# A five-layer decoder block on one core: turns from a list rule instead of fixed lags, and a memory layer with its probabilities normalised on GpSimd and its values loaded as column tiles

## The chip, the core and the metric

The kernel runs on one core of one Trainium2 chip. The metric is the device time of one execution in microseconds. Three runs of the kernel before took 1000.18, 1001.05 and 1002.54 us; their median is 1001.05 us.

## The reference, cut to what matters

```
x = x + attention(layernorm(x))                # 16 heads of 128, over the sequence: about half of the time
x = x + linear_attention(layernorm(x), ctx)    # "lin": relu features, 16 heads of 16, 64 context tokens
x = x + ffn(layernorm(x))                      # "ffn": silu, 704 hidden, 4-bit weights
x = x + feature_attention(layernorm(x))        # "fat": 256 x 256 energy, softmax
x = x + memory_attention(layernorm(x), ctx)    # "mem": the layer that the change rewrites
x = x + ternary_ffn(layernorm(x))              # "ter": 1024 hidden, relu squared, rounded to 255 steps

# memory_attention, per batch: 256 tokens, 16 heads of 16, 64 memory tokens
attn = softmax(where(mask, q @ k.T * scale, -inf))     # [16 heads, 256, 64]
out  = sigmoid(x @ wg.T) * ((attn @ v) @ wo.T)
# quantized relu2, per token: h = relu(h)**2; hmax = max(h, eps); h = round(h / hmax * 255) / 255 * hmax
```

x is 8 batches of 256 tokens of 256 features in float32.

## The kernel before, in words

The program has two parts with a barrier between them. `attention_part` does the first layer for all batches and prepares weights; it ends at about 560 us of the span. The change touches only one thing in it (two small memsets on GpSimd). `streams_part` does the other five layers. From its start on, batches don't need each other.

`streams_part` treats four batches at a time, as four streams. Each stream has buffers of its own (`xn_stream`, `xt_stream`, `big_stream`, `mid_stream` and others) and two of the eight PSUM banks, PA and PB. A loop (`Fori`) of two rounds does batches 0 to 3 and then 4 to 7. A round begins on DVE with the stage `copy` (L1392), which copies the batch from X into `x_stream`.

The order of the work is a list of stages written out by hand, one list for all layers. A stage is a small step of one batch, on one or more engines. `in_turns` goes through time slots, and in each slot the four streams come in turn, stream s being `LAGS[s]` = 0, 3, 6 or 9 slots behind stream 0. Each engine issues its own instructions in this order and waits on semaphores in it, so an instruction that waits holds up all that stands behind it on its engine. Since a round ends with the last stage of stream 3, no engine starts a stage of batches 4 to 7 before its last stage of batches 0 to 3.

The steps that the change and the prediction speak of, each per batch and, in mem and ter, per tile t of 128 tokens (two tiles for a batch, one after the other):

- norm of every layer: statistics on DVE (L1353, L1359, L1368), a power of -1/2 on GpSimd (L1222), the normalised x on DVE (L1373), four transposes on PE (L1554).
- `mem s`: two mask matmuls over 128 rows (L1670), then four score matmuls over 64 rows each (L1675); pairs of these use the upper and the lower half of the rows and write different banks.
- `mem max`, `sub` (DVE, L1479 and L1482), `exp` (ScalarE, L1304), `pt` (eight transposes on PE, L1683), `pte` (ScalarE, L1308).
- `mem o`: eight matmuls (L1689), with a 128x128 block of the probabilities as weights and 34 columns of v1 (two heads of 16, each with a column of ones for the row sum) moving.
- `mem rd`, `on` (DVE, L1486 and L1490): one over the row sum, and the product with it; then, once per batch, `mem ot` (four transposes on PE, L1554), `ote` (ScalarE, L1312) and `out` (four matmuls on PE, L1546).
- `ter h` (PE, L1704), `max` (DVE, L1498), `m0`, `m1`, `c0`, `c` (five small operations on DVE, L1502 to L1515), relu and square (ScalarE, L1317 and L1322), `r` and `n` (DVE, L1519 and L1522: round, and back to a float16 number), `nt` (PE, L1711), `nte` (ScalarE, L1326), `out` (PE, L1717), `add` (DVE, L1526).
- the output of a batch is a DMA from `x_stream` on the queue of SP (L1207).

A float32 matmul shows as two records in the trace, and so do its weight loads; the counts of L1675, L1689 and L1546 are twice the number of matmuls in the code.

## Time and profile before

| | |
|---|---|
| the profiled execution, its own time | 998.32 us |
| its span, first to last instruction | 996.5 us |
| mean granted clock of TensorE | 0.967 of 2.4 GHz |
| attention part, 0 to 560 us | not changed but for the memsets |
| streams part, 560 to 996.5 us | two rounds: the first ends at about 780 us |
| PE, DVE, ScalarE, GpSimd busy over the span | 912.4, 714.6, 506.8, 338.1 us |

The windows view cuts the streams part into stretches and gives the busy time of each engine in each. The two rounds run the same work, and their stretches can be laid side by side: 572 to 671 and 792 to 889 hold lin, ffn, fat and the start of mem, 671 to 728 and 889 to 946 the rest of mem, 728 to 780 and 946 to 996.5 the ternary layer.

### The profile page before, as it was taken

Reading aid. Unit: us, or ns where it says so; the run is one execution under the profiler, and the core shown is the slowest. Engines: PE = TensorE matmul, PEld = TensorE weight load, DVE = VectorE, ACT = ScalarE, POOL = GpSimd, SP = SyncE. Lnnn points to the kernel's source line nnn. Section 1 sums busy time; section 2 is a strip of 40 time slices with the busy share of each in tenths; the row PEclk is TensorE's granted clock in tenths of the full one; section 3 lists DMA queues with packets and bytes.
Section 4 is the critical chain, followed back from the end, with each engine's and each line's share of the span. In section 5 each row is a group of like instructions: output and inputs, shape, how many; then the busy total and the mean of one; then the engine's idle time right before and its main releaser. Section 6 shows DMA issues by size and latency. Waiting matters only on the chain. (4 is left out here: it accounts for less than half of the span.)

```text
span 996.5 us, 18805 instructions
## 1 busy us (share of the span) xinstructions
PE 912.4 (92%) x6772; PEld 685.7 (69%) x6772; DVE 714.6 (72%) x1785; ACT 506.8 (51%) x1219; POOL 338.1 (34%) x342
## 2 busy tenths in 40 slices
PE   5788999999999999999999599999877699999966
PEld 3556677777777777777777488787754488787843
DVE  6738778788887889878764447775588438775586
ACT  1445586666665666655664233533437224444455
POOL 3105455554554555554464302510010303410000
PEclk9799999999999999999999799999999699999998
DMA  8023131111001111001000000000000000000001
GB/s 270 22 61 79 21 93 33 33 32 32 8 24 32 32 32 32 8 24 32 11 1 1 1 1 2 1 1 1 1 1 22 23 1 1 1 1 1 1 1 43
DMA packets 34438, 25.27 MB, mean 25 GB/s; under 512 B 9332, under 2 KB 31436, under 8 KB 34380
## 3 DMA queue, kind: packets, MB, share of 16 engines
q1 hardware_dynamic: 34092, 24.23, 9.1%
q8 instruction: 36, 0.59, 0.2%
q10 hardware_dynamic: 288, 0.26, 0.1%
q14 instruction: 22, 0.18, 0.1%
HBM read 22.32 MB, written 2.17 MB: 25 GB/s over the span
## 5 line engine op out<-in xcount | busy, mean ns | idle before, releaser
L73 PE MATMUL banks<-value_out_hi,xn_t_hi 128*128 128x256 f16 x512 | 140.3, 274 | 2.3 <-DVE X L837 2.3
L572 ACT ACTIVATE exp_scores<-banks,exp_bias,unscale 128x256 f32<-128x256 f32 x256 | 141.0, 560 | 2.1
L468 POOL CAST exp_hi<-exp_scores 128x1024 f16<-128x1024 f32 x64 | 67.0, 1046 | 216.8 <-ACT exp_scores L572 216.8
L75 PE MATMUL banks<-value_out_hi,xn_t_lo 128*128 128x256 f16 x512 | 140.3, 274 | 0.0
L74 PE MATMUL banks<-value_out_lo,xn_t_hi 128*128 128x256 f16 x512 | 140.3, 274 | 0.0
L470 POOL TENSOR_TENSOR exp_lo<-exp_scores,exp_hi 128x1024 f16<-128x1024 f32 x64 | 138.3, 2160 | 5.1
L1222 POOL TENSOR_TENSOR rstd_stream<-rstd_stream,neg_half 128x2 f32<-128x2 f32 x40 | 29.5, 738 | 314.6 <-DVE rstd_stream L1368 279.2
L1009 PE MATMUL banks<-qk 128*128 128x256 f32 x512 | 121.4, 380 | 6.1 <-ACT exp_scores L572 6.0
L1009 PEld LDWEIGHTS banks<-qk 128*128 128x128 f32 x512 | 96.8, 190 | 26.7 <-issue 7.9
L837 DVE SCALAR_TENSOR_TENSOR X<-banks,colsum,X 128x256 f32<-128x256 f32 x256 | 106.2, 478 | 11.0 <-DVE colsum L828 9.6
L554 ACT ACTIVATE qk<-banks 128x512 f32<-128x512 f32 x128 | 75.8, 598 | 60.8 <-PE banks L75 60.7
L816 DVE TENSOR_REDUCE neg_rowmax<-banks 128x4 f32<-128x1024 f32 x64 | 78.2, 1222 | 29.9 <-PE banks L1009 29.9
L73 PE MATMUL banks<-xn_t_hi,head_weights_hi 128*128 128x512 f16 x256 | 96.9, 378 | 0.6 <-issue 0.6
L75 PE MATMUL banks<-xn_t_hi,head_weights_lo 128*128 128x512 f16 x256 | 97.0, 379 | 0.0
L74 PE MATMUL banks<-xn_t_lo,head_weights_hi 128*128 128x512 f16 x256 | 96.9, 379 | 0.0
L568 ACT ACTIVATE exp_bias<-neg_rowmax,unscale 128x4 f32<-128x4 f32 x64 | 18.8, 293 | 100.9 <-DVE neg_rowmax L816 100.9
L74 PEld LDWEIGHTS banks<-value_out_lo,xn_t_hi 128*128 128x128 f16 x512 | 50.3, 98 | 12.0
L73 PEld LDWEIGHTS banks<-value_out_hi,xn_t_hi 128*128 128x128 f16 x512 | 50.3, 98 | 11.2 <-DVE X L837 4.5
L75 PEld LDWEIGHTS banks<-value_out_hi,xn_t_lo 128*128 128x128 f16 x512 | 50.4, 98 | 6.0
L572 ACT ACTIVATION_READ_ACCUMULATOR exp_scores<-banks,exp_bias,unscale 128x1 f32 x256 | 50.8, 198 | 0.0
L1554 PE MATMUL banks<-ident,xn_stream 128*128 128x128 f32 x224 | 36.3, 287 | 14.3 <-DVE xn_stream L1373 14.3
L420 POOL TENSOR_TENSOR head_weights_lo<-head_weights,head_weights_hi 128x512 f16<-128x512 f32 x32 | 38.9, 1216 | 29.5 <-ACT head_weights_hi L486 29.4
(222 smaller groups left out, 1971.6 us busy)
## 6 DMA issues: line engine op xcount, KB each, us to landing
head_weights<-in_wqkv_d SPq DMA_DIRECT2D x32, 128.0 KB, 3.6
weight_absmax_rows<-across_partitions SPq DMA_DIRECT2D x15, 256.0 KB, 4.0
X<-in_x_d SPq DMA_DIRECT2D x4, 512.0 KB, 6.8
head_weights<-in_wqkvt_d SPq DMA_DIRECT2D x16, 128.0 KB, 3.4
head_weights<-in_w_o_d SPq DMA_DIRECT2D x16, 128.0 KB, 3.4
out<-x_stream SPq DMA_DIRECT2D x8, 256.0 KB, 2.1
features_then_ternary<-in_c_fc_d SPq DMA_DIRECT2D x1, 1024.0 KB, 5.6
features_then_ternary<-in_c_proj_d SPq DMA_DIRECT2D x1, 1024.0 KB, 7.3
```

What stands on the lines that cost most here:

```text
L73: nc.tensor.matmul(out, lhs[0], rhs[0], start=first, stop=False)
L74: nc.tensor.matmul(out, lhs[0], rhs[1], start=False, stop=False)
L75: return nc.tensor.matmul(out, lhs[1], rhs[0], start=False, stop=last)
L420: nc.gpsimd.tensor_tensor(wlo[:, u, 2 * a:2 * a + 2], wst[:, u, 2 * a:2 * a + 2], whi[:, u, 2 * a:2 * a + 2], ALU.subtract).then_inc(wlo_r ...
L468: nc.gpsimd.tensor_copy(probh[:, s1_.par], prob[:, s1_.par]).then_inc(exph_ready, 1)
L470: nc.gpsimd.tensor_tensor(probl[:, s1_.par], prob[:, s1_.par], probh[:, s1_.par], ALU.subtract).then_inc(expl_ready, 1)
L554: nc.scalar.activation(qk[:, st.par, s, :], qk_ps[s], ACT.Copy).then_inc(qk_ready, 1)
L572: last = nc.scalar.activation(prob[:, s1_.par, t, :], sc_ps[t // ST][:, t % ST, :], ACT.Exp, bias=nbias[:, t:t + 1], scale=unscale[:, s1_. ...
L816: nc.vector.tensor_reduce(nmax[:, :], sc_both, AX.X, ALU.max, negate=True).then_inc(nmax_ready, 1)
L837: last = nc.vector.scalar_tensor_tensor(out=g.X[:, TP * s2.p + t, :], in0=xm_ps[t // ST][:, t % ST, :], scalar=csum[:, t:t + 1], in1=g.X[: ...
L1009: last = nc.tensor.matmul(sc_ps[b][:, t, :], qk[:, s1_.par, 0, q], qk[:, s1_.par, 1, kk], start=True, stop=True)
L1554: last = nc.tensor.transpose(tiles(bank[s])[:, k, t * P:(t + 1) * P], xn[s][:, t, k * P:(k + 1) * P], g.ident[:, :])
```

## The change

Nine things are done; the first three are about order, the others about work.

1. The loop of two rounds is written out: all eight batches stand in one sequence, on all engines. Batches b and b + 4 share a set of buffers and two PSUM banks.
2. The order is no longer slots with lags but comes from `turns_by_engine`. It takes the list `work` (each step with its engine, a length written into it, and what it needs), and places the steps one by one: always the one that can start earliest by these lengths; of those that can start at the same time, the one with the longest chain still ahead of it, plus `LEAD` = 5.0 us for each stream place ahead, and with batches 0 to 3 ahead of 4 to 7. On each engine, batch b keeps behind batch b - 1 step by step, and batch b + 4 starts when the last step of batch b is done.
3. Steps that had been joined into one slot are placed one by one (in ffn above all).
4. Batches are worked on in place in X: the stage `copy` is gone.
5. mem: the probabilities are summed on DVE (`sum`, new), and multiplied by one over the sum on GpSimd (`pn`, new), before they are transposed. The column of ones in v1 and its memsets are gone.
6. mem: `o` has v1 as weights, 128x32 for two heads, and the probabilities move, 128 columns; the eight matmuls write four groups of 32 partitions of PA. So their result comes out transposed: `mem on` on DVE and `mem ot` on PE are gone. ScalarE moves it out, once per tile instead of once per batch.
7. mem: each mask matmul takes 64 rows instead of 128, one half of the rows for each bank.
8. ter: `m1`, `r` and one of the small operations' places are gone; the scale goes into the square on ScalarE, and `n` rounds and comes back in one operation with two additions.
9. SP, like the rest, waits on constants; the output DMA goes from X.

```diff
-LAGS = (0, 3, 6, 9)
+ENGINES = ("PE", "DVE", "ACT", "POOL")
+HOP, LEAD = 0.15, 5.0
...
-        for a in range(2):
-            if a:
-                pool.wait_ge(v1_ones, 1)
-            nc.gpsimd.memset(g.v1[a * M:(a + 1) * M, :, :, a, XD:XD + 1], 1.0).then_inc(v1_ones, 1)
-        pool.wait_ge(v1_ones, 2)
 
         for p in range(1, NP):
...
-    xs = sb("x_stream", [P, ST, D])
+    xs = [g.X[:, ST * b:ST * (b + 1), :] for b in R]
...
-    NORM = ["stats", "aggr", "eps", "xn", "turn", "xt", "lo"]
-    named = lambda layer, parts: [" ".join(f"{layer}_{k}" for k in p.split()) for p in parts]
...
+
+
+    NORM = ["stats", "aggr", "eps", "xn", "lo"]
+    def norm_work(layer, after, more):
+
+        return [f"{layer}_stats DVE .75 {after}", f"{layer}_aggr DVE .25", f"{layer}_eps DVE .11", f"{layer}_pow POOL .79",
+                f"{layer}_xn DVE .78", f"{layer}_turn PE .47"] + [f"{layer}_{w}" for w in more]
...
+    work += norm_work("mem", "fat_add", ["xt ACT .85"])
+    work += ["mem_q PE 1.74", "mem_kbd DVE .68 fat_add", "mem_g PE 1.74 mem_xt", "mem_qt ACT .6 mem_q", "mem_ge ACT .6 mem_g"]
     for t in range(ST):
-        stages += named(f"mem{t}", MEM_SLOTS)
-    stages += ["mem_ot", "mem_ote", "mem_out", "mem_go", "mem_add"]
-    stages += norm_stages("ter")
+        work += [f"mem{t}_{w}" for w in ("s PE 1.33" + (" mem_qt mem_kbd mem_ge" if t == 0 else ""),
+                                         "max DVE 1.17", "sub DVE 1.15", "exp ACT 1.05", "sum DVE 1.17", "rd DVE .2",
+                                         "pn POOL 2.2", "pt PE .92", "pte ACT 1.02", "o PE .75", "ote ACT .36")]
+    work += ["mem_out PE 1.74", "mem_go DVE .63", "mem_add DVE .63"]
+    work += norm_work("ter", "mem_add", ["xt ACT .6", "lo DVE .68"])
-        stages += named(f"ter{t}", TER_SLOTS)
-    stages += ["store"]
-
-    def in_turns(stage):
-
-        for slot in range(len(stages) + LAGS[-1]):
-            for s in R:
-                if 0 <= slot - LAGS[s] < len(stages):
-                    for name in stages[slot - LAGS[s]].split():
-                        layer, _, part = name.partition("_")
-                        stage(s, name, layer, part)
-
-    def numbers(eng, it):
-
-        return [eng.snap(it * STREAMS + (s + 1)) for s in R]
-
-    def tile_numbers(eng, it):
-
-        return [eng.snap(it * FFT + (m + 1)) for m in range(FFT)]
-
+        work += [f"ter{t}_{w}" for w in ("h PE 1.72" + (" ter0_nte ter0_add" if t else ""), "max DVE 1.17", "m0 DVE .2",
+                                         f"relu ACT 1.1 ter{t}_max", f"c0 DVE .3 ter{t}_m0", "c1 DVE .16",
+                                         f"sq ACT 1.05 ter{t}_relu ter{t}_c1", "n DVE .63", "nt PE .55", "nte ACT 1.01",
+                                         "out PE .87", "add DVE .42")]
+    turns = turns_by_engine(work)
+
+    def in_turns(eng, stage):
+
+        for b, name in turns[eng]:
+            layer, _, part = name.partition("_")
+            stage(b, name, layer, part)
...
+            elif part == "pn":
+                t = tile_of(layer)
+                pool.wait_ge(mem_rden[t], n[s])
+                nc.gpsimd.tensor_tensor(by_head(s), by_head(s), den[s][:, t, :].unsqueeze(2).broadcast_to([P, XH, M]),
+                                        ALU.mult).then_inc(mem_pn[t], 1)
...
+            elif layer in ("mem0", "mem1") and part == "ote":
+
+                t = tile_of(layer)
+                act.wait_ge(mem_o_full[t], n[s])
+                nc.scalar.activation(ot[s][:, :, t * P:(t + 1) * P], PA[s][:, 0:KT * P].rearrange("p (k n) -> p k n", k=KT),
+                                     ACT.Copy, scale=g.anykey[:, s:s + 1]).then_inc(mem_o[t], 1)
...
-                                                   op0=ALU.mult, op1=ALU.mult).then_inc(mem_o[t], 1)
...
-                elif part == "r":
-                    dve.wait_ge(ter_step[s], it * (5 * ST) + (5 * t + 5))
-                    dve.wait_ge(ter_sq[t], n[s])
-                    nc.vector.tensor_scalar(hid[s], hid[s], small[s][:, 8:9], ROUND, ALU.mult, ALU.add).then_inc(ter_r[t], 1)
-                elif part == "n":
-                    dve.wait_ge(ter_r[t], n[s])
-                    nc.vector.tensor_scalar(num[s], hid[s], -ROUND, None, ALU.add).then_inc(ter_n[t], 1)
...
+            elif part == "sum":
+                dve.wait_ge(mem_exp[t], n[s])
+                nc.vector.tensor_reduce(den[s][:, t, :], by_head(s), AX.X, ALU.add).then_inc(mem_sum[t], 1)
+            elif part == "rd":
+                dve.wait_ge(mem_sum[t], n[s])
+                nc.vector.reciprocal(den[s][:, t, :], den[s][:, t, :]).then_inc(mem_rden[t], 1)
...
+            elif part == "m0":
+                dve.wait_ge(ter_max[t], n[s])
+                nc.vector.tensor_scalar(small[s][:, 5:6], small[s][:, 4:5], g.tscale[:, 0:1], float(np.sqrt(1e-5)),
+                                        ALU.mult, ALU.max).then_inc(ter_step[s], 1)
+            elif part == "c0":
+                dve.wait_ge(ter_step[s], s // STREAMS * 3 * ST + 3 * t + 1)
+                nc.vector.reciprocal(small[s][:, 6:7], small[s][:, 5:6]).then_inc(ter_step[s], 1)
+                nc.vector.tensor_scalar(small[s][:, 9 + t:10 + t], small[s][:, 5:6], small[s][:, 5:6],
+                                        g.tscale255[:, 0:1], ALU.mult, ALU.mult).then_inc(ter_step[s], 1)
+            elif part == "c1":
+                dve.wait_ge(ter_step[s], s // STREAMS * 3 * ST + 3 * t + 2)
+                nc.vector.tensor_scalar(small[s][:, 7:8], small[s][:, 6:7], float(np.sqrt(255.0)), None,
+                                        ALU.mult).then_inc(ter_scale[t], 1)
+            elif part == "n":
+                dve.wait_ge(ter_sq[t], n[s])
+                nc.vector.tensor_scalar(num[s], hid[s], ROUND, -ROUND, ALU.add, ALU.add).then_inc(ter_n[t], 1)
...
+                for bank, rows in zip((PA[s], PB[s]), row_tiles):
+                    nc.tensor.matmul(bank.rearrange("p (h m) -> p h m", m=M), g.ones[rows, :],
+                                     g.maskb[rows, s:s + 1, :].broadcast_to([P // 2, HK, M]),
...
+            elif part == "o":
+                pe.wait_ge(mem_pt[t], n[s])
+                for j in range(XH // 2):
+                    rows = slice(j % 4 * 2 * XD, (j % 4 + 1) * 2 * XD)
+                    last = nc.tensor.matmul(PA[s][rows, j // 4 * P:(j // 4 + 1) * P],
+                                            g.v1[:, s, j].rearrange("p a e -> p (a e)"), pt[s][:, j * P:(j + 1) * P],
+                                            start=True, stop=True)
...
+def turns_by_engine(work):
+
+
+
+
+
+    names, engine, length, after = [], [], [], []
+    made = {}
+    for i, line in enumerate(work):
+        name, eng, took, *before = line.split()
+        names.append(name)
+        engine.append(eng)
+        length.append(float(took))
+        after.append([j for d in before or names[-2:-1] for j in made[d]])
+        made.setdefault(name, []).append(i)
+    users = [[j for j in range(len(work)) if i in after[j]] for i in range(len(work))]
+    rest = [0.0] * len(work)
+    for i in reversed(range(len(work))):
+        rest[i] = length[i] + HOP + max([rest[j] for j in users[i]], default=0.0)
+    own = {e: [i for i in range(len(work)) if engine[i] == e] for e in ENGINES}
+    urgency = lambda b, i: rest[i] + (max(rest) if b < STREAMS else 0.0) + LEAD * (STREAMS - b % STREAMS)
+    free = {e: 0.0 for e in ENGINES}
+    nth = {(b, e): 0 for b in range(B) for e in ENGINES}
+    done = {}
+    turns = {e: [] for e in ENGINES}
+    for _ in range(B * len(work)):
+        best = None
+        for b in range(B):
+            for e in ENGINES:
+                if nth[b, e] == len(own[e]):
+                    continue
+                i = own[e][nth[b, e]]
+                needs = [(b, j) for j in after[i]]
+                if b >= STREAMS:
+                    needs.append((b - STREAMS, len(work) - 1))
+                if b and nth[b - 1, e] <= nth[b, e] or any(x not in done for x in needs):
+                    continue
+                start = max([free[e]] + [done[x] for x in needs])
+                if best is None or (start, -urgency(b, i)) < best[0]:
+                    best = (start, -urgency(b, i)), b, e, i
+        (start, _), b, e, i = best
+        free[e] = start + length[i]
+        done[b, i] = free[e] + HOP
+        nth[b, e] += 1
+        turns[e].append((b, names[i]))
+    return turns
 
...
     g.kv0 = sb("kv0", [P, B, XH // 2, 34])
     g.k1t = sb("k1_t", [P, KT, B * M])
-    g.v1 = sb("v1", [P, B, XH // 2, 2, XD + 1])
+    g.v1 = sb("v1", [P, B, XH // 2, 2, XD])
```

## Rows read from the trace of the kernel before

**Rows 1.** The page, part 1: busy us and share of the span of each engine.
```profile
PE 912.4 (92%) x6772; PEld 685.7 (69%) x6772; DVE 714.6 (72%) x1785; ACT 506.8 (51%) x1219; POOL 338.1 (34%) x342
```

**Rows 2.** Windows of the streams part: busy us and count by engine, PE clock.
```profile
728.00:780.00 52.00, 34.73 (x223) 20.38 (x221) 38.20 (x102) 27.22 (x29) 2.46 (x3) 0.90 0.07 22
...
792.00:889.00 97.00, 95.70 (x685) 79.94 (x684) 66.61 (x194) 40.04 (x101) 25.62 (x37) 0.98 0.00 1
889.00:946.00 57.00, 53.81 (x373) 44.02 (x372) 32.92 (x61) 23.18 (x30) 2.06 (x3) 1.00 0.00 1
946.00:996.50 50.50, 33.67 (x216) 19.80 (x214) 37.38 (x96) 26.94 (x28) 1.95 (x3) 0.88 0.06 22
```

**Rows 3.** Timeline from one round of the loop to the next.
```profile
766.05 11.62 SPq L1207 DMA_DIRECT2D out<-x_stream  x4
...
776.64 0.48 DVE L1526 SCALAR_TENSOR_TENSOR x_stream<-banks,small_stream,x_stream 128x256 f32<-128x256 f32 x1 [3.04 <-PE banks L1717]
779.98 0.43 DVE L1392 COPY x_stream<-X 128x512 f32 x1 [2.85 <-issue]
...
783.40 1.11 PE L1554 MATMUL banks<-ident,xn_stream 128*128 128x128 f32 x4 [6.86 <-DVE xn_stream L1373]
...
785.20 3.78 PE L1539 MATMUL banks<-xt_stream,wq 128*128 128x256 f32 x8 [0.69 <-ACT xt_stream L1249]
```

**Rows 4.** Windows over the same place.
```profile
764.00:772.00 8.00, 4.62 (x39) 2.65 (x37) 6.51 (x20) 6.16 (x6) 0.00 (x0) 1.00 0.19 65
772.00:788.00 16.00, 7.34 (x35) 5.19 (x36) 7.33 (x24) 1.62 (x2) 4.08 (x4) 0.54 0.11 36
788.00:792.00 4.00, 3.93 (x19) 2.78 (x18) 2.10 (x8) 2.03 (x4) 2.16 (x3) 0.71 0.00 0
```

**Rows 5.** Timeline of a score stage, and of a turn before an output product.
```profile
671.13 0.59 PE L1670 MATMUL banks<-mask_bias,ones 128*128 x2
...
671.65 0.73 PEld L1675 LDWEIGHTS banks<-big_stream,qt_stream 64*128 64x128 f32 x8 [0.42 <-issue]
671.65 1.13 PE L1675 MATMUL banks<-big_stream,qt_stream 64*128 64x256 f32 x8
672.72 0.94 PEld L1539 LDWEIGHTS banks<-xt_stream,wq 128*128 128x128 f32 x5 [0.33 <-issue]
...
727.02 0.64 PE L1554 MATMUL banks<-ident,xn_stream 128*128 128x128 f32 x4
...
727.49 1.68 PE L1546 MATMUL banks<-wo,ot_stream 128*128 128x256 f32 x7
```

**Rows 6.** Three pieces of the chain that ended last: start, us, what.
```profile
671.72 1.06 PE banks L1675 x8
...
674.71 1.74 PE banks L1546 x8
...
683.95 1.71 PE banks L1689 x16
```

**Rows 7.** Groups of the streams part by line, and L470 from the page.
```profile
L1222 POOL TENSOR_TENSOR rstd_stream<-rstd_stream,neg_half 128x2 f32<-128x2 f32 x40 | 29.5, 738 | 314.6 <-DVE rstd_stream L1368 279.2 <-DVE rstd_stream L1365 35.4
...
L1479 DVE TENSOR_REDUCE den_stream<-banks 128x16 f32<-128x1024 f32 x16 | 19.6, 1225 | 22.2 <-PE banks L1675 22.2
...
L1519 DVE TENSOR_SCALAR big_stream<-big_stream,small_stream 128x1024 f32<-128x1024 f32 x16 | 12.0, 751 | 3.0 <-ACT big_stream L1322 2.5
...
L1233 POOL TENSOR_TENSOR x_stream<-x_stream,bo 128x512 f32<-128x512 f32 x8 | 10.8, 1350 | 9.3 <-DVE xn_stream L1373 9.3
...
L1252 ACT ACTIVATE xt_stream<-banks,normw 128x256 f32<-128x256 f32 x16 | 6.7, 472 | 0.0
...
L1490 DVE SCALAR_TENSOR_TENSOR xn_stream<-banks,any_key,den_stream 128x256 f32<-128x256 f32 x16 | 7.4, 462 | 0.0
...
L470 POOL TENSOR_TENSOR exp_lo<-exp_scores,exp_hi 128x1024 f16<-128x1024 f32 x64 | 138.3, 2160 | 5.1
```

**Rows 8.** Waits of PE in the streams part: total, times, longest.
```profile
PE banks L1554 <- DVE xn_stream L1373: 14.3, 4, 6.9
```

More of the change, by code:

```diff
@@ new lines, in streams_part @@
+    for place in range(2 * FFT + 3):
+        for back, part in enumerate(("ab PE .87", "tanh ACT .36", "u DVE .36", "h DVE .42", "hi ACT .36", "lo POOL .68")):
+            m = tile_at(place - back)
+            if m is not None:
+                name, length = part.split(" ", 1)
+                before = f"ffn_{('lo', 'ab', 'tanh', 'u', 'h', 'hi')[back]}"
+                after = f"{before}{m}" if back else "ffn_lo" if m < 2 else f"ffn_h{m - 2}"
+                work += [f"ffn_{name}{m} {length} {after}"]
@@ L1212, in _ @@
+        sp.wait_ge(stored, 16 * B)
     @block.gpsimd
     def _(pool):
[L1214 to L1236 removed]
@@ L1330, in _ @@
+        in_turns("ACT", stage)
     @block.vector
@@ L1533, in _ @@
+        in_turns("DVE", stage)
     @block.tensor
```

850 lines of the change are left out of this document (392 added, 458 removed).

## The prediction

> **What bounds the kernel now.** I read the page's busy times first. PE leads with 912.4 of 996.5 us, DVE follows with 714.6 [rows 1]. A share over the whole span says little here, since the change acts on the 436 us after 560 us alone, so I cut those into windows by layer. The reader is to see three kinds of stretch in them. In lin, ffn and fat PE is busy 95.7 of 97.0 us: PE sets the pace, DVE has a third of its time free, and no order of turns can win more than 1.3 us there. In the memory layer PE is busy 53.8 of 57.0 us and DVE 32.9: PE still sets the pace. In the ternary layer nobody is full: PE 34.7 of 52.0 and 33.7 of 50.5 us, DVE 38.2 and 37.4 [rows 2]. There each of four batches walks down a long chain, and DVE is the engine most in demand. The stretches of the other round are like these.
>
> Then I read the place between the rounds in the timeline. The first batch's output leaves at 766.05, the last add of the round is at 776.64, the copy of batch 4 begins at 779.98 (2.85 us of this wait is put down to no other engine), its first transposes at 783.40 after 6.86 us of waiting, and its query product takes 3.78 us from 785.20 [rows 3] against 1.74 us for a product of the same eight records later [rows 6]. The windows say why: the granted clock is 0.54 from 772 to 788, close to the 1.2 GHz level, and 0.71 in the 4 us after it [rows 4]. So the change of rounds costs idle time and then slow time. The waits of PE agree: 14.3 us in only 4 waits go to normalised inputs that are late, the longest 6.9 us [rows 8].
>
> **Order of turns and one sequence.** Batch 4 may start when batch 0 is done, 14 us before it does now (766.05 against 779.98), so its lin work falls into the end of the ternary layer. How much is that worth? From 764 to 792 PE is busy 4.6, 7.3 and 3.9 us at clocks of 1.00, 0.54 and 0.71 [rows 4]; at full clock that is 4.6 + 4.0 + 2.8 = 11.4 us of work in 28 us. DVE is busy 6.5 + 7.3 + 2.1 = 15.9 us there; four copies of 0.43 and about two of the removed rounding operations (0.95, below) come off, 12.3 us stay, and at 88% of DVE that is 14 us. DVE decides, and the stretch saves **14 us**. From 728 to 764 nothing overlaps yet, but six tiles drop 0.95 us of DVE each, 5.7 us; I take **4 us**. Together 18; bounds 10 (batch 0 finishes only just before batch 3, since all four go nearly in step) and 26 (DVE no limit: 28 - 11.4/0.95 = 16, and more in the ternary layer, where 17.3 of 52.0 us of PE are idle).
>
> What is queued behind what: the new order is as fixed as the old one, and on each engine an operation that is late holds up the others. I cost this at nothing in lin, ffn and fat, where PE's queue is full and hides it; with the cover gone it costs what the order places wrongly, which nothing here bounds but the 1.3 us that PE idles now on one side and the ternary layer's rate of idling (a third) on the other. The copy of the first batch was ahead of everything at 560 us: **1 us** (0.43 and a hop). The other copies were covered by PE. The two memsets of v1's ones on GpSimd lie early in the attention part with nobody waiting: 0. SP still issues eight output DMAs; only the last one counts, as now.
>
> **The memory layer on PE**, per tile, 16 tiles:
> - Values. Before: 1.71 us for eight matmuls, 0.214 us each, of which only the weight loads can be the reason, since just 34 columns move [rows 6]. After: 128 columns move; a matmul of 256 columns costs 1.74/4 = 0.43 us, so 128 cost 0.22. The trace has no column tiles, but it has row tiles: four score matmuls of 256 columns take 1.06 us where four whole ones take 1.74 [rows 6], so pairs run side by side at 2 x 0.43 + 0.20. If four column tiles do the same, eight matmuls take 2 x 0.22 + 0.3 for going in and out of the tiled form = 0.75 us, and 0.96 us are saved. If they don't, they take 8 x 0.22 + 0.3 = 2.05 and 0.34 are lost. I take the side of the row tiles, the nearest row: 16 x 0.96 = 15.4 us.
> - Turning the result: 727.49 - 727.02 = 0.47 us [rows 5], 8 times, 3.8 us.
> - Masks: two one behind the other are 671.65 - 671.13 = 0.52 us [rows 5]; side by side half, so 16 x 0.26 = 4.2 us, less the entry into the row form, which stays; 3.4 us.
> Sum 22.6 us of PE work, 11.3 us in each round's memory window.
>
> What a change of form costs stands in the same rows. The weight load of the scores waits 0.42 us, that of the next stage 0.33 us [rows 5], but the matmuls themselves start 0.52 us after the masks, where the two masks alone need 2 x 0.21, so I count 0.1 in and 0.2 out. The Trainium skill (TensorEngine Tiling (Array Packing), Key Properties) says that changing the tiling mode drains TensorE, and each value stage adds two such changes. With the whole 0.42 + 0.33 us charged, a value stage takes 0.44 + 0.75 = 1.19 us, 7 us less is saved in all, and the time would be 966 us instead of 959.
>
> **The memory layer on DVE, ScalarE, GpSimd.** DVE gains `sum`, like the maximum over 128x1024, 1.22 us, and loses the product `on`, 0.46 [rows 7]: +0.76 x 8 = 6.1 us a window, 32.9 + 6.1 = 39 us. ScalarE gains a second evacuation: one more 256-column move, at most 16 x 0.47 = 7.5 us [rows 7] even with the old one counted at nothing, on an engine half free [rows 1]. GpSimd gains `pn`, 128x1024 in float32: 2.16 us like L470 or 2 x 1.35 = 2.7 us like L1233 [rows 7]; 8 x 2.7 = 22 us in a window where it does nearly nothing. But `pn` and `sum` lie in the chain of a tile: about 1.22 + 2.7 + two hops more, about 0.96 + 0.47 less. And behind a `pn` on GpSimd's queue stand the 0.74 us powers of other batches' norms, which can be 2.7 us late. Four batches must hide a chain that is some 2.5 us longer per tile, with PE's work down to 53.8 - 11.3 = 42.5 us and DVE's at 39. PE fills 94% of this window now and 67% of the ternary one; I take 88%, nearer the first since PE is still the fullest: 42.5/0.88 = 48.3, a gain of 8.7 us, **18 us** in two rounds. Bounds 2 and 24 (42.5/0.94 = 45).
>
> **The ternary layer.** `r` (0.75 us, L1519 [rows 7]) and one small operation of about 0.2 us go from each tile's chain. In the last window DVE loses 8 x 0.95 = 7.6 us; the last batch's own chain loses 2 x 0.95 = 1.9. Between them: **5 us**, bounds 2 and 8.
>
> **Sum.** 18 + 1 + 18 + 5 = 42 us. The profiled execution took 998.32 us with a span of 996.5; 998.3 - 42 = 956.3. The median of the runs is 1001.05, 2.7 us above it, so **959 us**.
>
> **Rivals.**
> - The memory layer gives nothing, since column tiles run one by one (2.05 us a stage) or the longer chain through GpSimd starves PE. PE's work falls only by 16 x (0.21 - 0.34) + 3.8, about 2 us. 2 + 18 + 1 + 5 = 26: 975 us, 970 to 982. For it: no row shows a column tile, and DVE comes close to PE. Against: row tiles do overlap, and GpSimd idles. Chance 0.14. The drain counted in full lies between this and the forecast and is part of neither; by the rows half of it is hidden. Chance 0.08, 966 us.
> - Every place fills up: memory windows at 94% (24), the change of rounds 26, last window 8, head 1: 59 us, 942 us, 932 to 948. For it: PE's idle time now lies almost only where the four batches end or begin, and one sequence could close that. Against: a batch waits for the whole of the one whose buffers it takes. Chance 0.22.
> - No overlap between the rounds, since the order keeps the four in step and batch 0 ends late: 10 instead of 18, 967 us. Chance 0.06.
> - Slower: the clock. After 6.9 us of PE idle time the granted clock is near half, and a product takes 3.78 us instead of 1.74 [rows 3, 4]. If the lighter memory layer leaves PE gaps in which its clock falls to 1.2 GHz, the work done there takes twice as long. Each microsecond of PE work at the lower level costs one more; with 42 us gained, it decides from 42 us on, that is one of the two memory windows whole. Both whole would give 959 + 85 = 1044 us. For it: in the ternary layer, PE at 67%, the clock is 0.90 and 0.88 [rows 2]. Against: most of that fall lies at the ends of those windows, and the gaps in between are only of 1 to 3 us. Chance 0.04.
> - The forecast, 949 to 965 us around 959: chance 0.46.
>
> **How the numbers follow.** The range 940 to 980 takes in the forecast, most of both neighbours and the full drain, and leaves out some 0.16: the far side of the good rival, the end of the bad one, and the slower one. Within 0.2% (2 us) of before is no change that can be measured; faster 0.95, the same 0.01, slower 0.04.
>
> **What the profile after would show.** Value stages of 0.75 us, four matmuls side by side, and no transposes behind them; if 2 us, the tiles run one by one. `pn` at 2.2 to 2.7 us. In the memory windows PE at 85 to 90% and DVE near 80%. No idle stretch of PE above 3 us in the middle of the streams part, the clock at 1.0 there, lin work of batch 4 between ternary work of batches 1 to 3. The last window some 45 us. The prediction is wrong if the fixed order meets lengths that the chip doesn't have: then PE waits 1 us and more, often, in lin, ffn and fat too, where it has no idle time now.

## The result, and the profile after

Four runs of the changed kernel took 964.23 to 969.64 us, median 966.02; four of the kernel before on the same chip had a median of 1000.62. The ratio is 0.9656 with a 95% interval of 0.9622 to 0.969: faster by 34.6 us. The forecast was 959, with 949 to 965 for its own case and 940 to 980 for the range. It was 7 us too low, inside the range and 1 us outside its own case. The profiled execution took 967.47 us, its span is 965.7 us, 30.8 less than before.

The page's busy times answer to [rows 1]. PE's fell by 24 us, DVE's rose by 10:

```profile
span 965.7 us, 18389 instructions
PE 888.5 (92%) x6740; PEld 662.4 (69%) x6740; DVE 724.2 (75%) x1745; ACT 508.9 (53%) x1227; POOL 367.7 (38%) x356
```

To see where the time came from I cut both spans at the same events: the first score matmul of a round's memory layer, the last gated add of that layer, and the last add of the ternary layer.

| stretch | before | after | gained | forecast |
|---|---|---|---|---|
| start of the span to the first scores | 671.7 | 673.3 | -1.6 | 1 |
| memory layer, batches 0 to 3 | 65.4 | 63.7 | 1.7 | 9 |
| from there to the scores of batch 4 | 152.8 | 130.1 | 22.7 | 18 |
| memory layer, batches 4 to 7 | 63.8 | 62.1 | 1.7 | 9 |
| from there to the last ternary add | 39.5 | 33.4 | 6.1 | 5 |
| after it | 3.3 | 3.1 | 0.2 | 0 |

The windows view of the kernel after answers to [rows 2] and [rows 4]. A row gives the stretch and its length, then the busy times of PE, weight loads, DVE, ScalarE and GpSimd (with counts), the granted clock, the DMA share and GB/s; the sixth row comes from the same view with the instructions of L1565 alone and leaves the other engines out:

```profile
673.30:737.00 63.70, 53.37 (x412) 38.61 (x408) 57.34 (x97) 30.50 (x43) 19.04 (x13) 0.95 0.00 1
867.10:929.20 62.10, 51.84 (x412) 37.78 (x408) 57.17 (x96) 30.24 (x43) 19.04 (x13) 0.97 0.00 1
...
572.00:673.30 101.30, 100.74 (x688) 83.31 (x689) 64.53 (x181) 40.26 (x101) 25.50 (x37) 0.94 0.00 1
...
750.00:780.00 30.00, 27.57 (x216) 21.29 (x213) 21.30 (x66) 19.40 (x27) 6.92 (x7) 1.00 0.11 36
...
800.00:810.00 10.00, 9.69 (x50) 8.65 (x49) 4.14 (x13) 1.06 (x2) 0.70 (x1) 0.66 0.00 0
...
800.00:810.00 10.00, 5.03 (x32) 4.92 (x32) 0.66 0.00 0
```

In the memory layer the bound has changed hands. PE is at 84% and 83%, and DVE at 90% and 92%. DVE is busy 57 us between these events. Before, it was 39.6 there, and the 6.1 us that the forecast adds (to 32.9 in its shorter window) would make it 45.7. At the change of rounds the long idle time is gone: from 750 to 780 PE is busy 27.57 of 30 us at full clock.

The timeline of the kernel after shows both (start, length, engine, line and tiles; in brackets the idle time before it):

```profile
698.50 0.39 PE L1642 MATMUL banks<-mask_bias,ones 64*128 64x512 bf16 x2 [0.75 <-ACT gate_stream L1297]
698.71 1.04 PE L1647 MATMUL banks<-big_stream,qt_stream 64*128 64x256 f32 x8
...
699.68 0.64 PE L1662 MATMUL banks<-mid_stream,v 128*32 128x128 f32 x16
...
700.26 1.09 PE L1655 MATMUL banks<-ident,big_stream 128*128 128x128 f32 x8
...
709.79 1.90 POOL L1229 TENSOR_TENSOR big_stream<-big_stream,den_stream 128x1024 f32<-128x1024 f32 x1 [1.58 <-DVE den_stream L1479]
710.33 1.92 DVE L1458 SCALAR_TENSOR_TENSOR X<-gate_stream,X 128x512 f32<-128x512 f32 x1
...
728.04 1.12 PE L1534 MATMUL banks<-ident,xn_stream 128*128 128x128 f32 x4 [1.96 <-DVE xn_stream L1371]
730.57 3.59 PE L1677 MATMUL banks<-ternary,xt_stream 128*128 128x512 f16 x8 [0.41 <-DVE xt_stream L1376]
...
752.99 0.74 DVE L1351 BATCH_NORM_STATS2 stats_stream<-X 128x6 f32<-128x256 f32 x2
...
758.59 0.60 PE L1534 MATMUL banks<-ident,xn_stream 128*128 128x128 f32 x4
758.87 0.48 DVE L1506 SCALAR_TENSOR_TENSOR X<-banks,small_stream,X 128x256 f32<-128x256 f32 x1 [0.32 <-PE banks L1690]
...
760.11 1.13 PE L1519 MATMUL banks<-xt_stream,wq 128*128 128x256 f32 x4
```

A value stage (L1662) takes 0.58 us from its start to that of the next stage, where eight matmuls took 1.71 [rows 6]. Masks and scores take 1.18 us (698.50 to 699.68) against 1.59 (671.13 to 672.72 in [rows 5]). Batch 4's statistics begin at 752.99, its transposes and query product at 758.59 and 760.11, among ternary adds of the first round (L1506), the last of which begins at 776.5. Before, the copy came 3.3 us after the start of the last of them [rows 3]. And at 710.33 lies what the prediction doesn't have: a gated add on DVE takes 1.92 us, where it took 0.686 before. It ends 0.56 us after the product `pn` on GpSimd that was running when it began. This is one gated add in four; the other three of the round meet no `pn` and take 0.68.

The two lines from 728 on show a second price. A variance operation at 723.68 takes 1.27 us beside a `pn` that runs from 723.03, and the normalised x behind it is late. PE is busy only 1.19 us from 724 to 728 and 3.56 from 728 to 732. The granted clock is 0.98, then 0.50, then 0.74 until 737, and eight ternary products (L1677) take 3.59 us where the same eight at 722.20 took 1.90. Round two has the same place at 922, with 0.57 from 922 to 926.

The groups view of the streams part (total busy, mean ns of one, then the idle time before them) gives the sizes; the first two rows answer to [rows 7]:

```profile
L1229 POOL TENSOR_TENSOR big_stream<-big_stream,den_stream 128x1024 f32<-128x1024 f32 x16 | 30.4, 1907 | 48.0 <-DVE den_stream L1479 48.0
L1476 DVE TENSOR_REDUCE den_stream<-big_stream 128x16 f32<-128x1024 f32 x16 | 19.2, 1200 | 1.5 <-ACT big_stream L1301 1.5
...
L1366 DVE TENSOR_SCALAR rstd_stream<-mv_stream 128x2 f32<-128x2 f32 x32 | 11.9, 373 | 0.3
...
L1662 PE MATMUL banks<-mid_stream,v 128*32 128x128 f32 x256 | 11.2, 296 | 2.4 <-ACT mid_stream L1305 2.3
...
L1447 DVE TENSOR_TENSOR big_stream<-k_t,headmask 128x256 f32<-128x256 f32 x16 | 9.3, 620 | 0.0
L1458 DVE SCALAR_TENSOR_TENSOR X<-gate_stream,X 128x512 f32<-128x512 f32 x8 | 7.9, 991 | 0.1
```

`pn` takes 1.91 us, less than forecast. But the variance operation of 128x2 elements (L1366) has a mean of 373 ns where it had 169, the key blocks (L1447) 620 against 420, the gated add (L1458) 991 against 686: DVE instructions that the change didn't touch, all longer.

The waits of PE (total, times, longest) answer to [rows 8]:

```profile
PE banks L1534 <- DVE xn_stream L1371: 12.9, 6, 6.9
PE banks L1690 <- ACT mid_stream L1327: 8.0, 10, 1.1
PE banks L1655 <- POOL big_stream L1229: 4.1, 4, 1.2
```

The 6.9 us are now those of the start of the streams part, ending at 567.6. After it no wait of PE is longer than 1.96 us.

### The profile page after: what moved, and what is told of

It is laid out like the page before. It is cut to its first block and busy times, and to the rows that moved or that the text cites. A ratio compares the mean times of both kernels' runs of the same rounds, so it can differ in the third digit from the quotient of the medians.

```text
span 965.7 us, 18389 instructions
## 1 busy us (share of the span) xinstructions
PE 888.5 (92%) x6740; PEld 662.4 (69%) x6740; DVE 724.2 (75%) x1745; ACT 508.9 (53%) x1227; POOL 367.7 (38%) x356
## 5 line engine op out<-in xcount | busy, mean ns | idle before, releaser
L74 PEld LDWEIGHTS banks<-value_out_hi,xn_t_hi 128*128 128x128 f16 x512 | 50.3, 98 | 11.2 <-DVE X L830 4.5
L1229 POOL TENSOR_TENSOR big_stream<-big_stream,den_stream 128x1024 f32<-128x1024 f32 x16 | 30.4, 1907 | 48.0 <-DVE den_stream L1479 48.0
```

The costliest lines, as they stand in the source:

```text
L74: nc.tensor.matmul(out, lhs[0], rhs[0], start=first, stop=False)
```

## The experiments

All are edits of the changed kernel, and all ratios are to runs of the kernel before on the same chip. The median of the kernel before lay between 999.94 and 1003.25 us beside these kernels, with single runs from 994.8 to 1006.8. So differences between two kernels are given by medians, and by ratios where these say something else. A difference of a few microseconds between two kernels isn't told apart from nothing.

### Which part of the change gives how much

**The order alone.** The memory layer of before, with its own work list and lengths, in the new order; the rest as changed.

```diff
-                       "max DVE 1.17", "sub DVE 1.15", "exp ACT 1.05", "sum DVE 1.17", "rd DVE .2",
-                       "pn POOL 2.2", "pt PE .92", "pte ACT 1.02", "o PE .75", "ote ACT .36")]
-    work += ["mem_out PE 1.74", "mem_go DVE .63", "mem_add DVE .63"]
+                       "max DVE 1.17", "sub DVE 1.15", "exp ACT 1.05",
+                       "pt PE .92", "pte ACT 1.02", "o PE 1.71", "rd DVE .26", "on DVE .46")]
+    work += ["mem_ot PE .47", "mem_ote ACT .6", "mem_out PE 1.74", "mem_go DVE .63", "mem_add DVE .63"]
...
```

> The changed kernel with the memory layer of before (ones column in v1, product and turn behind the values, masks over 128 rows); order, one sequence, work in place and ternary layer as changed. Theory A (the memory layer's saving on PE is mostly lost because DVE becomes its bound, the join of the rounds gives what the prediction said): 1000.6 - 18 - 5 - 1 = 977 us, 973 to 981, so the new memory layer is worth 7 to 15 us. Theory B (the memory layer gives all of its 18 us, and the order loses elsewhere): 984 us or more. Theory C (the memory layer gives nothing): 966 to 969 us.

982.87 us (974.13 to 983.63), ratio 0.9788 [0.9726, 0.9851], between the ranges of theories A and B. In the new order the rewrite is worth 16.9 us by medians and 13 by ratios. Its window of the second memory stretch:

```profile
874.30:943.70 69.40, 66.49 (x427) 53.18 (x426) 44.82 (x94) 29.15 (x39) 3.48 (x5) 0.95 0.00 1
```

The stretch is 69.4 us long, not 63.8: the list rule brings work of the neighbouring layers into it (427 matmul records against 394 between the same events before, and 5.2 us of DVE's work), and PE is at 96%. So the table above hides the rewrite's gain: in the new order it takes this stretch from 69.4 to 62.1.

**The work alone.** The changed work in the old slots and lags, in two rounds one after the other.

```diff
-    turns = turns_by_engine(work)
+    turns = turns_by_slots(work)
+def turns_by_slots(work):
+    ...
+        slots += [f"mem{t}_{p}" for p in ("s", "max", "sub", "exp", "sum rd", "pn", "pt", "pte", "o", "ote")]
+    ...
+    lags = (0, 3, 6, 9)
+    for first in range(0, B, STREAMS):
+        for slot in range(len(slots) + lags[-1]):
+            ...
```

> The changed kernel's work, written out and in place, but its turns by the slots and lags 0, 3, 6, 9 of before, in two rounds one behind the other (sum and reciprocal, GpSimd's product and the evacuation have slots of their own). Theory A: the memory layer gives about 10, the ternary one 8 in two rounds, the copies 1, the join of the rounds nothing: 1000.6 - 19 = 982 us, 977 to 987. Theory B (the list rule hurts outside the join): 970 us or less. If the join is worth less than thought, also near 972.

987.77 us (985.02 to 988.38), ratio 0.9863 [0.9824, 0.9902], just above theory A's range: 12.2 us by the median of before beside it, 1000.01, and 13.7 by the ratio. The memory stretches are 59.9 and 58.7 us:

```profile
883.80:942.50 58.70, 47.56 (x379) 35.83 (x376) 47.20 (x77) 26.56 (x37) 18.03 (x12) 0.94 0.00 1
```

In the old slots `pn` hardly meets the operations that it holds up elsewhere: the means are 184 ns for the variance operation, 420 for the key blocks and 682 for the gated add; only the normalisation is longer, 496 against 456. DVE is at 80%, as forecast. Even so the two stretches gain only 5.5 and 5.1 us where the forecast had 8.7 each. PE is at 81% and not at 88%, at a granted clock of 0.91 and 0.94. So the forecast's share of 88% for PE was too high here with hardly any hold-ups; the longer chain and the clock are left as causes, and no run separates them. By medians the changed work as a whole, with the ternary layer's part, is worth more in the new order (16.9 and 2.3 us, below); by ratios (13 and 3) the difference is small.

**No overlap of the rounds.** Batches 4 to 7 start when batch 3 is done instead of batch b - 4; all else as changed.

```diff
-                    needs.append((b - STREAMS, len(work) - 1))
+                    needs.append((STREAMS - 1, len(work) - 1))
```

> The changed kernel with one edit in the list rule: batches 4 to 7 may start only when batch 3 is done, not each when the batch of its buffers is. Theory A (overlap of the rounds is worth 14 us or so): 966 + 14 = 980 us, 976 to 985. Rival (batch 0 ends only just before batch 3, so little overlaps): 967 to 972 us.

982.15 us (981.98 to 982.53), ratio 0.9806 [0.9768, 0.9845]. The overlap is worth 16.1 us (15 by ratios), and what else the list rule does is worth less: with the rounds apart it is 5.6 us ahead of the old slots.

**The ternary layer of before**, put back into the changed kernel (`m1`, `r` and the older scale back).

```diff
-                                         f"sq ACT 1.05 ter{t}_relu ter{t}_c1", "n DVE .63", "nt PE .55", "nte ACT 1.01",
+                                         f"r DVE .75 ter{t}_sq ter{t}_c1", "n DVE .63", "nt PE .55", "nte ACT 1.01",
...
-                nc.vector.tensor_scalar(num[s], hid[s], ROUND, -ROUND, ALU.add, ALU.add).then_inc(ter_n[t], 1)
+                nc.vector.tensor_scalar(hid[s], hid[s], small[s][:, 8:9], ROUND, ALU.mult, ALU.add).then_inc(ter_r[t], 1)
```

> The changed kernel with the ternary layer of before (m1, rounding and conversion as two operations, square without scale), placed by the same list rule. Theory A (the removed 0.95 us of DVE for a tile is worth 5 at the end and 4 at the join): 975 us, 971 to 978. Rival (worth only the last batch's chain, 1.9 us, once or twice, as the window of the slots kernel suggests with 1.8 us a round): 968 to 970 us.

968.3 us (967.36 to 970.32), ratio 0.9684 [0.9633, 0.9734], with a span of 965.6 us. That is 2.3 us above 966.0 (3 by ratios), which the intervals don't separate. The time saved on DVE doesn't show; that other batches' work hides it is the likely reading.

### The column tiles

**One group.** All eight value products write partitions 0 to 31, so they have no groups to run side by side in. ScalarE still moves out all of PA, so the layer's result is left wrong.

```diff
-                    rows = slice(j % 4 * 2 * XD, (j % 4 + 1) * 2 * XD)
-                    last = nc.tensor.matmul(PA[s][rows, j // 4 * P:(j // 4 + 1) * P],
+                    last = nc.tensor.matmul((PA, PB)[j // 4][s][0:2 * XD, j % 4 * P:(j % 4 + 1) * P],
```

> The changed kernel, but all eight value matmuls write partitions 0 to 31 (four blocks of columns in PA, four in PB) instead of four groups of 32 partitions; the output of the layer isn't the reference's. Theory (the four column tiles run side by side): the value stage goes from 0.7 us to 8 x 0.22 + 0.3 = 2.05 us, PE's busy time rises by about 20 us, and PE at 52 + 11 = 63 us a memory stretch becomes its bound again: 970 to 980 us. Rival (tiles don't run side by side even now, 0.7 us comes from something else): stage and time unchanged, 964 to 968 us.

983.32 us (977.96 to 985.8), ratio 0.9781 [0.974, 0.9822], 17.3 us above the changed kernel (12.5 by ratios) and 3 above the range expected. The groups view of this kernel:

```profile
L1661 PE MATMUL banks<-mid_stream,v 128*32 128x128 f32 x256 | 33.3, 287 | 2.2 <-ACT mid_stream L1305 2.2
```

33.3 us in 16 stages are 2.08 us each, where the changed kernel has 11.2/16 = 0.70. A single matmul record takes the same in both (287 and 296 ns); they run four side by side or not.

### What DVE lost

**`pn` only writes.** GpSimd writes ones into a spare tile for as long as `pn` lasted, instead of multiplying; the probabilities stay unnormalised.

```diff
+    spare = sb("spare", [P, 2176])
...
-                nc.gpsimd.tensor_tensor(by_head(s), by_head(s), den[s][:, t, :].unsqueeze(2).broadcast_to([P, XH, M]),
-                                        ALU.mult).then_inc(mem_pn[t], 1)
+                nc.gpsimd.memset(spare[s][:, :], 1.0).then_inc(mem_pn[t], 1)
```

> The changed kernel, but in place of the product on GpSimd stands a memset of 128x2176 numbers of a spare tile on GpSimd, of the same length (about 1.91 us each); the probabilities stay unnormalised. Chain and GpSimd's load are the same, only GpSimd's reads are gone. Theory A1 (GpSimd's reads hold up DVE operations that take two inputs from SBUF or go from SBUF to SBUF; DVE is the bound of the memory layer): the variance operation falls back from a mean of 373 ns to 170, the gated add from 991 to 690, the key blocks from 620 to 420, DVE's busy time falls by 13 us or so and the time is 954 to 960 us. Theory A2 (the hold-ups lie in the shadow of other waits): durations fall, time 963 to 967 us. Theory A3 (any GpSimd operation holds DVE up, writing too): durations stay and so does the time.

956.31 us (956.02 to 957.35), ratio 0.9532 [0.9508, 0.9556]: 9.7 us faster (12 by ratios) at the same length of the operation on GpSimd. Its groups:

```profile
L1230 POOL MEMSET spare<- 128x2176 f32 x16 | 30.5, 1912 | 45.3 <-DVE den_stream L1479 45.3
L1476 DVE TENSOR_REDUCE den_stream<-big_stream 128x16 f32<-128x1024 f32 x16 | 19.3, 1206 | 1.5 <-ACT big_stream L1301 1.5
L1366 DVE TENSOR_SCALAR rstd_stream<-mv_stream 128x2 f32<-128x2 f32 x32 | 11.9, 374 | 0.3
L1458 DVE SCALAR_TENSOR_TENSOR X<-gate_stream,X 128x512 f32<-128x512 f32 x8 | 6.4, 803 | 0.1
L1447 DVE TENSOR_TENSOR big_stream<-k_t,headmask 128x256 f32<-128x256 f32 x16 | 5.9, 407 | 0.0
```

The key blocks, which have two inputs in SBUF, get back all of their time (407 ns), and the gated add much of it (803). The variance operation, a `tensor_scalar` with one input, doesn't (374), and neither does the normalisation, another one: 502 ns and 503, where it had 456 before the change. So the hold-ups are real, but what GpSimd reads is only part of them. The two gated adds that are still long (1.15 us, six others take 0.68 or 0.69) stand right behind a variance operation. It starts at 720.54 beside a memset from 719.87 to 721.78 and ends at 721.80; the add starts at 720.66 and ends at 721.81. So it seems to wait behind the variance operation, not for GpSimd itself.

The Trainium skill ("SBUF — State Buffer", section "Who interferes with whom") says that DVE and GpSimd share a pair of ports under an exclusive lock: a DVE instruction with two SBUF inputs contends with a GpSimd instruction that reads SBUF and not with one that only writes, `tensor_scalar` can contend when it runs in a mode that takes both ports, `tensor_reduce` never. The trace agrees on all three, with 620 to 407, 373 to 374, and 1200 to 1206 ns; in which mode `tensor_scalar` ran it doesn't show.

The windows view says where the 9.7 us come from. Both memory stretches are 57.7 us, 6.0 and 4.4 less than in the changed kernel:

```profile
860.60:918.30 57.70, 50.31 (x412) 37.36 (x408) 53.05 (x96) 30.22 (x43) 18.67 (x13) 1.00 0.00 1
```

The list of work and so the order are the same. DVE is 4.3 and 4.1 us less busy and still at 92%, and the granted clock is 1.00 where it was 0.95 and 0.97. So the gain lies in the memory stretches, and most of it is DVE's time.

**`pn` on DVE.** The same product, on DVE behind the reciprocal.

```diff
-                       "pn POOL 2.2", "pt PE .92", "pte ACT 1.02", "o PE .75", "ote ACT .36")]
+                       "pn DVE 1.2", "pt PE .92", "pte ACT 1.02", "o PE .75", "ote ACT .36")]
...
+            elif part == "pn":
+                dve.wait_ge(mem_rden[t], n[s])
+                nc.vector.tensor_tensor(by_head(s), by_head(s), ...
```

> The changed kernel with the product by one over the sum on DVE (about 1.22 us) instead of GpSimd (1.91 us). GpSimd does nothing in the way of DVE then, so the variance operation should be back at 0.17 us and the key blocks at 0.41. Theory A (DVE is the bound of the memory stretches; it gains 9.8 us of work a stretch and loses about 6 of hold-ups, the chain of a tile is 0.7 us shorter): 968 to 976 us. Rival (the hold-ups and the detour through GpSimd's queue cost more than the product): 956 to 964 us.

968.72 us (964.56 to 976.83), ratio 0.9708 [0.9643, 0.9773]: not told apart from the changed kernel. The groups:

```profile
L1361 DVE TENSOR_SCALAR rstd_stream<-mv_stream 128x2 f32<-128x2 f32 x32 | 6.5, 207 | 0.3
L1442 DVE TENSOR_TENSOR big_stream<-k_t,headmask 128x256 f32<-128x256 f32 x16 | 5.7, 400 | 0.0
L1453 DVE SCALAR_TENSOR_TENSOR X<-gate_stream,X 128x512 f32<-128x512 f32 x8 | 5.5, 684 | 0.1
```

With no long operation on GpSimd all three are at or near their old lengths. DVE pays 1.21 us per tile for the product instead. Moving it to GpSimd took 19 us off DVE's list and was worth 2.7 us by medians and 5 by ratios, neither clear of noise.

**One maximum per token.** One maximum over all heads, given to the exponential on ScalarE as a bias; the subtraction on DVE (1.22 us per tile) is gone. The softmax is the same as long as a token's heads don't differ so much in their maxima that their exponentials underflow.

```diff
-                act.wait_ge(mem_sub[t], n[s])
-                nc.scalar.activation(prob[s], prob[s], ACT.Exp).then_inc(mem_exp[t], 1)
+                act.wait_ge(mem_max[t], n[s])
+                nc.scalar.activation(prob[s], both[s].rearrange("p b n -> p (b n)"), ACT.Exp,
+                                     bias=small[s][:, 12 + t:13 + t]).then_inc(mem_exp[t], 1)
...
```

> The changed kernel, but in the memory layer one maximum per token over all 16 heads is taken off (softmax is the same for any shift), as the bias of the exponential on ScalarE, which reads PSUM; the subtraction on DVE (1.22 us, 16 times) is gone, 9.8 us of DVE for each memory stretch. Theory A (DVE bounds the memory layer, at 57 of 62 us): the stretch falls from 62 to about 56 us, where PE's 52 us take over, in two rounds 10 to 16 us: 950 to 956 us. Rival (the memory layer is bound by PE's order or by the length of the chain, which loses only 1.2 of some 14 us a tile): 961 to 965 us.

957.04 us (949.12 to 959.49), ratio 0.9549 [0.9523, 0.9574]: 9.0 us faster than the changed kernel (11 by ratios), and the fastest version here that leaves no part of the computation out. Its second memory stretch:

```profile
854.20:910.50 56.30, 49.37 (x412) 37.60 (x408) 44.29 (x89) 30.65 (x43) 18.71 (x13) 1.00 0.00 1
```

With 9.8 us of DVE work taken out, the stretch is 5.8 us shorter (62.1 to 56.3) and DVE's busy time 12.9 less, at 79%; PE is at 88%. The first stretch falls by as much (63.7 to 57.9). DVE was the bound there, and with room on it fewer of its instructions meet `pn` (the gated add is back at 686 ns, the variance operation at 270; the key blocks stay at 623). The profiled execution took 949.12 us, 7.9 less than this kernel's median, so its stretches may flatter it.

**One maximum, and the key blocks on GpSimd**, too. The edit of the work list, beside the one for the maximum:

```diff
-    work += ["mem_q PE 1.74", "mem_kbd DVE .68 fat_add", "mem_g PE 1.74 mem_xt", "mem_qt ACT .6 mem_q", "mem_ge ACT .6 mem_g"]
+    work += ["mem_q PE 1.74", "mem_kbd POOL 1.3 fat_add", "mem_g PE 1.74 mem_xt", "mem_qt ACT .6 mem_q", "mem_ge ACT .6 mem_g"]
...
```

> The kernel with one maximum per token, and besides the key blocks made on GpSimd (two products of 128x256, about 0.7 us each) instead of DVE (0.62 us each with the hold-ups, 16 times). Theory A (DVE still counts in the memory layer): another 3 to 6 us, 950 to 955 us. Rival (PE has taken over with one maximum, and the new reads of GpSimd hold DVE up elsewhere): 956 to 960 us, no gain.

957.44 us (956.16 to 958.05), ratio 0.9564 [0.9515, 0.9613]. No gain. GpSimd takes 626 ns for what took DVE 420 undisturbed. With one maximum DVE is no longer the fullest (79% against PE's 88%), so there was little left to win; that is argued, not tried.

### How much the order depends on its one number

`LEAD` is what an earlier stream place is worth in the choice between steps that can start together.

```diff
-HOP, LEAD = 0.15, 5.0
+HOP, LEAD = 0.15, 15.0
```

> The changed kernel with LEAD 15 instead of 5 us: streams are further apart, so that one batch's memory layer meets another's ffn, where DVE has room. Theory A (DVE's peak in the memory layer is the bound, since four batches are in it nearly in step): the memory layers lose 4 to 10 us in all, the last batch ends later behind the others by up to as much: 958 to 967 us. Rival (step doesn't matter, only the ends do): 970 to 985 us.

979.41 us (976.58 to 982.38), ratio 0.977 [0.9739, 0.9801]: 13.4 us slower than with 5.0, as the rival had it.

```diff
-HOP, LEAD = 0.15, 5.0
+HOP, LEAD = 0.15, 0.0
```

> The changed kernel with LEAD 0 instead of 5 us. At 15 us the time rose by about 11 us. Theory A (the ends count: batches that stop together leave less of PE idle at the end, but the next round's batches start later): within 962 to 970 us, no clear difference, so 5 is near a flat bottom. Rival (each us of lead costs as the step from 5 to 15 did, 1.1 us per us): 958 to 961 us.

1016.24 us (1015.12 to 1017.08), ratio 1.0152 [1.0101, 1.0203]: slower than the kernel before, and outside what either theory expected. The waits of PE in this kernel, and its windows, the first two of everything and the last two of the value products of lin (L1565) alone:

```profile
PE banks L1655 <- POOL big_stream L1229: 16.9, 6, 5.5
PE banks L1534 <- DVE xn_stream L1371: 14.5, 4, 7.9
PE banks L1684 <- DVE mid_stream L1502: 13.4, 7, 4.2
```

```profile
820.00:840.00 20.00, 20.00 (x89) 19.36 (x90) 4.09 (x15) 1.79 (x3) 0.00 (x0) 0.51 0.00 1
600.00:620.00 20.00, 20.00 (x95) 19.24 (x96) 6.35 (x21) 2.39 (x4) 0.71 (x1) 0.64 0.00 1
...
820.00:840.00 20.00, 14.48 (x68) 14.34 (x68) 0.51 0.00 1
600.00:620.00 20.00, 11.30 (x53) 11.16 (x53) 0.64 0.00 1
```

Without a lead the four batches arrive at each step together. PE waits 16.9 us for `pn` instead of 4.1 and 13.4 us for the ternary numbers instead of 1.9, and the granted clock is low in the value products of lin, which take 49.3 us in all instead of 31.5 (below).

And with one maximum per token, the lead raised a little:

```diff
-HOP, LEAD = 0.15, 5.0
+HOP, LEAD = 0.15, 8.0
```

> The kernel with one maximum per token, LEAD 8 instead of 5 us. Lead 0 cost 50 us, lead 15 some 11. Theory A (a smooth bottom between, 5 near it): 952 to 962 us, no clear difference from lead 5 with one maximum (957). Rival (each lead is an order of its own, and small changes of it move the time by 10 us and more either way, through where lin's value products of several batches come to lie): outside 950 to 965 us.

965.89 us (962.79 to 968.96), ratio 0.9651 [0.9618, 0.9684], 8.9 us slower than with 5.0 (10 by ratios), and outside theory A's range. A change of 3 us in a number that no engine executes costs as much as taking the subtraction off DVE had won. Lead 8 wasn't run without the one maximum.

## Why the prediction was right in its size and wrong in parts

- **Order and one sequence.** Right in mechanism, and by the table 22.7 us for 18. But part of it is paid back: the order brings other work into the memory stretches, which are 4.0 and 5.6 us longer with the old memory layer in them (69.4 against 65.4 and 63.8). By undoing it, the overlap is worth 16.1 us. The prediction took the gain for one of the place between the rounds alone; no term of it stood for work that is moved into another stretch. Two rivals gave nearly the right time for wrong reasons. Without overlap it was to be 967 us, but with the rounds apart the time is 982. With the full drain it was to be 966, and no stage shows that drain (see below).
- **The head.** Forecast 1 us won; 1.6 us were lost. The copy is gone, but PE's busy time in lin, ffn and fat of the first round rose from 98.4 us (572.0 to 671.7) to 100.7 (572.0 to 673.3) with the clock down from 0.98 to 0.94. PE is full there, as forecast, yet full at a lower clock.
- **The memory layer on PE.** Right, on the low side. Value stages are 0.70 us (forecast 0.75), 2.08 one by one (forecast 2.05); masks and scores gain 0.41 us a tile with their changes of form (forecast 0.21). The full drain of the rival with 966 us isn't there: it had 1.19 us a stage.
- **The memory layer on DVE: the step whose reading failed.** The forecast had DVE at 39 us in its window (45.7 between the events used here) and PE as "the fullest". DVE was busy 57.2 us in 62.1. Of the 17.6 us above the 39.6 of before (same events), 5.9 are `sum` less `on` (9.6 - 3.7), which was forecast; 5.2 are work of other layers, as with the order alone (44.8); the remaining 6.5 are hold-ups by `pn`. The mean lengths in this stretch bear that out: three variance operations at 1.05 us instead of 0.17, ten normalisations at 0.56 instead of 0.41, four key blocks at 0.83 instead of 0.42, three gated adds at 1.09 instead of 0.69 make 7.0 us. The prediction costed `pn` on GpSimd as 22 us "in a window where it does nearly nothing", and asked only who waits behind it on GpSimd's queue, not what runs beside it on DVE. The share of 88% for PE failed with it, and, as the old slots show (81%), not by the hold-ups alone.
- **What that cost.** The rewrite was worth 13 to 17 us in the new order, under the forecast's 18. That it came so near is partly luck: PE's side gave more than its term, and DVE's took more. Removing GpSimd's reads, or 9.8 us of DVE's work, gives 9.7 or 9.0 us more, and either would have met the forecast (956.3 and 957.0 against 959).
- **The clock.** The slower rival saw the mechanism: a lighter memory layer leaves PE gaps, and the clock falls. It does, to 0.50 and 0.57 behind the 1.96 us waits at 728 and 922, for some microseconds and not for a whole window. With these waits shorter (0.91 us, `pn` that only writes) the stretches had 1.00.
- **The ternary layer: the mis-sized terms.** Forecast 5 us, and 4 of the 18 from the same removed operations between 728 and 764. Undone, it is worth some 2.3 us. These two terms were each worked out as if the other part weren't there; what one sequence already hides can't be won a second time.
- **By cause**, then, in medians: memory rewrite 16.9 (18 forecast), ternary 2.3 (9), the rest, that is order and copy, 34.6 - 16.9 - 2.3 = 15.4 (15). By medians most of the 7 us between forecast and result is ternary work counted as if nothing hid it. By ratios it is 13, 3 and 18 for the rest, and the memory layer is short by 5 as well. Which of the two splits is right the runs don't settle.
- **Signs named for the profile after.** PE at 85 to 90% in the memory windows: 83 to 84%. DVE near 80%: 90 to 92%. `pn` at 2.2 to 2.7 us: 1.9. No idle time of PE above 3 us in the middle: so it is. Full clock there: yes from 750 to 780, but 0.50 from 728 to 732 and 0.66 from 800 to 810. No waits in lin, ffn and fat: 0.6 us of 101.3.

What stays open: why 5.0 is a good lead. The runs show 0 and 15 to be worse, and 8 with one maximum, not which step each of them misplaces. How much the longer chain of a tile costs by itself wasn't tried either.

## What to carry to other kernels

Work that is moved to an idle GpSimd isn't free for DVE: list the DVE instructions that will run beside it, above all `tensor_scalar` however small and those with two inputs in SBUF, and charge up to the GpSimd instruction's length for each that meets it (the worst here lost 1.6 of 1.9 us). When an order is changed so that stretches overlap, cost the savings by undoing each from the end state, since what is hidden is won once; and measure a kernel with a planned order at several values of the planner's own weights before trusting a difference of 1% in the work.

## What the runs showed of the hardware that wasn't expected

A `tensor_scalar` on DVE of 128x2 elements, 0.17 us by itself, took 1.05 us in the mean of three beside 1.9 us GpSimd products; a GpSimd memset of the same length, which reads nothing, left it as slow. Reductions on DVE kept their 1.20 us throughout.

TensorE's clock fell while PE showed no idle time. In the kernel with lead 0, PE was busy all of 800 to 810, at a clock of 1.00 and with nearly none of lin's value products. From 810 to 815 it did these alone, 5.00 us of 5, and the clock was 0.73, then 0.50. The granted clock was 0.51 from 820 to 840, near the 1.2 GHz level, with PE busy 20.00 of 20 us, 14.48 of them in lin's value products: 34 columns move per 128x128 block of weights, and the weight loads are as busy (19.36 us) as the matmuls. In 600 to 620 it was 0.64 with 11.30 us of them. The changed kernel has 5.03 us of them in 800 to 810 at a clock of 0.66. In 790 to 795 it has 3.66 us of them in 5 at 1.00. In 840 to 860, with none of them, lead 0 has PE busy only 17.8 of 20 us and a clock of 1.00. So a PE that the profile shows as full isn't always at full clock. The low clock came with long runs of these products; that spreading them out keeps it up wasn't tried by itself.
